# Layer 1's last sums on VectorE and GpSimd behind the last anchor tiles, their reads issued at once, and the anchors' rows read on ScalarE's queue

## The chip, the cores and the metric

The kernel runs on one core of a Trainium2 chip. The metric is the device time of one execution in microseconds (us). Before the change three executions took 1198.98, 1211.15 and 1212.76 us, with a median of 1211.15 us. A fourth execution, the profiled one, took 1202.78 us; its span from first to last instruction is 1200.6 us.

## What is computed

Two transformer layers run over x of shape (8, 256, 256), that is 2048 tokens of width 256. Each layer adds a cross-attention over 120 context rows and then a mixture of experts. Only the end of layer 1's mixture is touched by this change:

```python
# layer 1, per token of x (2048 tokens, 256 wide)
topidx = top 6 of 32 experts, tw = their normalised weights * 0.2
routed = sum over the 6 of tw * (silu(x @ w_gate[e]) * (x @ w_up[e])) @ w_down[e]
shared = silu(x @ shared_w_gate) * (x @ shared_w_up) @ shared_w_down
lg     = topidx[:, 0] // 2                        # one of 16 anchors
anchor = (silu(x @ anchor_w_gate[lg]) * (x @ anchor_w_up[lg])) @ anchor_w_down[lg]
out    = routed + shared + 0.1 * anchor
x      = x + out
```

So the last step adds to each token's row of x (which already holds the attention's and the shared expert's part) six rows of routed results and one row of the anchor's result.

## The kernel before

The program is written engine by engine, with every wait on a semaphore written out. Instructions of one engine run in the order of the code, and a wait holds up everything behind it on that engine. The tokens lie as 16 tiles of 128 (`NT = 16`) in the SBUF tile `X`, 256 numbers a token.

**Expert tiles.** Tokens of layer 1 are sorted by expert into tiles of 128 rows in DRAM (`buf1`). There are 160 such tiles (`NTL`): 128 routed ones and 32 of anchors. `tile_order` puts an anchor tile behind every fourth routed one from the 48th on and leaves 13 anchor tiles for the end. Index 146 is the last routed tile, `ROUTED` is 147, and indices 147 to 159 are anchors. For each tile i the loop does the following, each engine some tiles behind the one before:

- SyncE (SP) loads the tile's rows (`bx1_load`, `BX` or a piece of `R`), seven tiles ahead. The row's place comes from a table by a register load.
- TensorE (PE) transposes them (L304, L305). VectorE (DVE) copies the transpose to `XT` (L1410) and finds each row's destination `DI` and weight `WC` (`matches`, L1395 to L1403).
- PE multiplies by the gate and up weights (L656). ScalarE (ACT) applies silu (`SL`, L1134), DVE multiplies (`AC`, L1656), PE transposes (L665), ACT copies (`AT`, L1140), and PE multiplies by the down weights (L672).
- ACT scales the result by the weight (`yt_out`, L1087) into one of six buffers. GpSimd (POOL) scatters it by an indirect DMA (`put_back`, L884): rows of routed tiles go to `yb1` (six rows a token), those of anchor tiles to `yba` (one row a token).

**Last sums.** When all routed tiles are done (`all_back(E0 + ROUTED - 1)`), SP reads `yb1` back into SBUF with `yf_load(n)`, n from 0 to 7, each two token tiles (1.5 MB, 6 KB a row). The place `YF` is where the routed weights lay. From n = 4 on a read waits until DVE has done some of the sums. DVE runs `yf_add(n)` for one token tile in each step of the tile loop from i = 153 on, and the rest behind the loop: one addition of 768 numbers a partition, then three of 256. When all anchor results are in DRAM (`all_back(E0 + NTL - 1)`), SP reads them with four DMAs of 0.5 MB into `YA`. DVE adds them in four additions of 1024 numbers (L1666), and ACT writes each quarter of `X` out (L1145).

In the chip's trace the tiles `YF`, `YA`, `W1` and so on all bear the name `R`, since they are parts of one tensor. `yb1` is `yb` and `buf1` is `buf`.

Of the kernel before, what the change touches and what calls it, by code (L numbers as in the profile page):

```python
# [8 lines left out]
ALU = mybir.AluOpType  # L9
# [5 lines left out]
NT = 16  # L15
NB = 8
# [3 lines left out]
E0 = 64  # L20
# [9 lines left out]
EARLY = 3  # L30
NBX = 7
NYT = 6
BIG = 65536.0
SEG = 17
DUM = R1 * SEG
# [6 lines left out]
NTL = T1 + TA  # L42
# [45 lines left out]
ROUTED = ORDER.index(T1 - 1) + 1  # L88
# [15 lines left out]
class Chain:  # L104
# [14 lines left out]
    + [f"sc{i}" for i in range(6)] + ["z_b0", "z_y0", "z_dum"]  # L119
    + [f"ew{i}" for i in range(NEW // 2)] + [f"bx{i}" for i in range(NBX)] + [f"yt{i}" for i in range(NYT)]  # L120
    + [f"yl{i}" for i in range(3)] + [f"w1_{i}" for i in range(8)] + [f"wa_{i}" for i in range(4)]
    + ["pad_s", "pad_a", "pad_b"] + [f"yf{i}" for i in range(4)] + [f"ya{i}" for i in range(4)]

    + ["p_z", "p_va", "p_set", "p_y", "p_xc"]

    + ["s_kt", "s_tr", "s_q", "s_v", "s_s", "s_t", "s_o", "s_wo", "s_h2t", "s_rt", "s_ps"]
    + ["s_gu", "s_dn", "s_ta", "s_g", "s_t2", "s_y", "s_tot", "s_tab"]
# [3 lines left out]

    + ["dv", "d_ln", "d_h", "d_v", "d_cap", "d_mx", "d_pt", "d_cx", "d_x", "d_ln2", "d_hr", "d_lg", "d_sn", "d_sel", "d_ps"]
    + ["d_sum", "d_ri", "d_as", "d_add", "d_xt", "d_wc", "d_di", "d_ac", "d_kt", "d_bq", "d_xc", "d_tot", "d_pad", "d_cnt"]
    + ["d_tab", "d_te", "d_xf", "d_out"]
)


def build(nc, a, out):
# [10 lines left out]
    with ExitStack() as ctx:  # L149
# [11 lines left out]
        X = sb("X", [P, NT, D])  # L161
# [102 lines left out]
        YF = R[:, 0:NT * 1536].rearrange("p (s n) -> p s n", s=NT)  # L264
        YA = R[:, 24576:24576 + NT * D].rearrange("p (s n) -> p s n", s=NT)
# [7 lines left out]
        yv1p = yv1.rearrange("(n p) m -> p n m", p=P)  # L273
        yva = yba.rearrange("(n p) d -> p n d", p=P)
        buf1t = buf1.rearrange("(u p) r -> u p r", p=P)

        S = {name: ctx.enter_context(nc.semaphore(name)) for name in SIGNALS}
# [33 lines left out]
        def step(active):  # L311
            for g in list(active):
                if next(g, "end") == "end":
                    active.remove(g)
# [7 lines left out]
        def all_back(w, i):  # L322

            for k in range(i - NYT + 1, i + 1):
                s, n = result(k)
                w.wait_ge(f"yt{s}", 16 * n)
# [18 lines left out]
        def sweep(l, main, prepare, finish, first, behind, each=None):  # L345

            active = [first] if first is not None else []
            for u in range(-LEAD, NU + 2):
                if u % 4 == (-LEAD) % 4 and (u + LEAD) // 4 < NB:
                    active.append(prepare((u + LEAD) // 4))  # L350
                for slot in range(6):
                    main(u, slot)
                    if slot == 4 and u % 2 and 0 <= u - 2 < NU:
                        active.append(finish((u - 2) // 2, active))
                    step(active)
                    if u >= NU - 5 and slot % 2:
                        step(active)
                if each is not None and u > -LEAD + 1:
                    each()
            active.extend(behind)  # L360
            while active:
                step(active)

        block = ctx.enter_context(nc.Block())

# [311 lines left out]
        def _(e):  # L677
            w = Once(e, S)
# [127 lines left out]
            def yf_load(n):  # L806
                if n == 0:
                    w.wait_ge("s_y", E0 + ROUTED)
                    all_back(w, E0 + ROUTED - 1)
                e.dma_start(YF[:, 2 * n:2 * n + 2, :], yv1p[:, 2 * n:2 * n + 2, :]).then_inc(S[f"yf{n % 4}"], 16)  # L810

            for i in range(NBX):
                bx1_load(i)
            for i in range(NTL + 3):
                if i < 8:
                    pad(16 + 2 * i)
                if i + NBX < NTL:
                    bx1_load(i + NBX)
                if 10 <= i < 26:
                    pad(22 + i)  # L820
                n = i - ROUTED - 3
                if 0 <= n < NB:
                    if n >= 4:
                        w.wait_ge("d_xf", 2 * (n - 3))
                    yf_load(n)
            w.wait_ge("s_y", E0 + NTL)
            all_back(w, E0 + NTL - 1)
            for g in range(4):
                e.dma_start(YA[:, 4 * g:4 * g + 4, :], yva[:, 4 * g:4 * g + 4, :]).then_inc(S[f"ya{g}"], 16)


        @block.gpsimd
        def _(e):
            w = Once(e, S)
# [45 lines left out]
            def put_back(i, yb, bound):  # L880
                w.wait_ge("a_yt", i + 1)
                w.wait_ge("d_di", i + 1)
                j = i if i < E0 else i - E0
                e.indirect_dma_start(  # L884
                    out=yb[:, :], out_offset=bass.IndirectOffsetOnAxis(ap=DI[:, j:j + 1].bitcast(U32), axis=0),
                    in_=YTS[result(i)[0]], in_offset=None, bounds_check=bound, oob_is_err=False).then_inc(
                        S[f"yt{result(i)[0]}"], 16)
# [22 lines left out]
            for i in range(NTL):  # L910
                yb, bound = (yb1, 2048 * 6 - 1) if ORDER[i] < T1 else (yba, 2047)
                put_back(E0 + i, yb, bound)


        @block.scalar
        def _(e):
# [161 lines left out]
            def yt_out(i):  # L1078
                j = i if i < E0 else i - E0
                w.wait_ge("s_y", i + 1)  # L1080
                w.wait_ge("d_wc", i + 1)
                slot, n = result(i)
                if n > 1:
                    w.wait_ge(f"yt{slot}", 16 * (n - 1))
                if slot > 2:
                    w.wait_ge("s_dn", 4 * EARLY if i < E0 else 32)
                e.activation(YTS[slot], PS[:, 4 + j % 2, 0:256], ACT.Copy, scale=WC[:, j % 8:j % 8 + 1]).then_inc(  # L1087
                    S["a_yt"], 1)
# [35 lines left out]
            for i in range(NTL + 3):  # L1124
                if i in (0, 3):
                    w1_load(6 + i // 3)
                if i in (28, 32, 36, 40):
                    wa_load((i - 28) // 4)
                if 0 <= i - 1 < NTL:
                    j, wd = i - 1, width(i - 1)  # L1130
                    w.wait_ge("s_g", E0 + j + 1)
                    if j > 1:
                        w.wait_ge("d_ac", E0 + j - 1)
                    e.activation(SL[:, j % 2, 0:wd], PS[:, 2 + j % 2, 0:wd], ACT.Silu).then_inc(S["a_sl"], 1)  # L1134
                if 0 <= i - 2 < NTL:
                    j, wd = i - 2, width(i - 2)
                    w.wait_ge("s_t2", j + 1)
                    if j > 1:
                        w.wait_ge("s_y", E0 + j - 1)
                    e.copy(AT[0:wd, j % 2, :], PS[0:wd, 6 + j % 2, 0:P]).then_inc(S["a_at"], 1)  # L1140
                if 0 <= i - 3 < NTL:
                    yt_out(E0 + i - 3)
            for g in range(4):
                w.wait_ge("d_out", g + 1)
                e.dma_start(out_d[:, 4 * g:4 * g + 4, :], X[:, 4 * g:4 * g + 4, :]).then_inc(S["out"], 16)  # L1145
            w.wait_ge("out", 64)

# [2 lines left out]
        def _(e):  # L1150
# [479 lines left out]
            ready1 = set()  # L1630
            attention(1, route1, rows1, combine, [shared(1, 1, ready1, add1, range(4)), tables()], ready1, xc)

            def yf_add(n):
                yl = YF[:, n, :]
                w.wait_ge(f"yf{n // 2 % 4}", 16 * (n // 8 + 1))
                e.tensor_tensor(yl[:, 0:768], yl[:, 0:768], yl[:, 768:1536], ALU.add).then_inc(*dv.up())  # L1636
                t = dv.n
                w.wait_ge("dv", t)
                w.wait_ge("d_add", 32)
                e.tensor_tensor(X[:, n, :], X[:, n, :], yl[:, 512:768], ALU.add).then_inc(*dv.up())  # L1640
                e.tensor_tensor(yl[:, 0:256], yl[:, 0:256], yl[:, 256:512], ALU.add).then_inc(*dv.up())  # L1641
                w.wait_ge("dv", dv.n)
                e.tensor_tensor(X[:, n, :], X[:, n, :], yl[:, 0:256], ALU.add).then_inc(S["d_xf"], 1)

            w.wait_ge("d_tab", 1)
            for i in range(NTL + 3):
                if i < NTL:
                    xt_copy(E0 + i)
                    w.wait_ge(f"bx{(E0 + i) % NBX}", 16 * ((E0 + i) // NBX + 1))
                    matches(E0 + i, TE[:, ORDER[i]:ORDER[i] + 1])  # L1650
                if 0 <= i - 1 < NTL:
                    j, wd = i - 1, width(i - 1)
                    w.wait_ge("a_sl", E0 + j + 1)
                    if j > 1:
                        w.wait_ge("s_t2", j - 1)
                    e.tensor_tensor(AC[:, j % 2, 0:wd], SL[:, j % 2, 0:wd], PS[:, 2 + j % 2, wd:2 * wd], ALU.mult).then_inc(  # L1656
                        S["d_ac"], 1)
                if ROUTED + 6 <= i:
                    yf_add(i - ROUTED - 6)
            for n in range(NTL + 3 - ROUTED - 6, NT):  # L1660
                yf_add(n)
            for g in range(4):
                ns = slice(4 * g, 4 * g + 4)
                w.wait_ge(f"ya{g}", 16)
                w.wait_ge("d_xf", 4 * g + 4)
                e.tensor_tensor(X[:, ns, :], X[:, ns, :], YA[:, ns, :], ALU.add).then_inc(S["d_out"], 1)  # L1666

def by_partition(gate, up, down=None):

# [43 lines left out]
```

## Time and profile before

| | |
|---|---|
| three executions | 1198.98, 1211.15, 1212.76 us (median 1211.15) |
| profiled execution | 1202.78 us, span 1200.6 us |
| mean granted TensorE clock | 0.853 of full speed |
| busy in the span: PE, DVE, POOL, ACT | 81%, 55%, 44%, 41% |
| last slice of 30 us: DVE, DMA engines | 8 tenths, 7 tenths |

How to read the rows further down: times are microseconds from the span's start. A row of the timeline gives the start, the duration, the engine, the line of the code, the operation, and what is written `<-` what is read. In square brackets it gives how long the engine was idle before, and what ended that. A name like SPq or ACTq is the engine's queue issuing a DMA. PEclk is the TensorE clock granted, as a share of full speed.

### The profile page before, as it was taken

To read this page: it belongs to the slowest core of one execution; us is meant where nothing else is said; L and a number is where in the kernel's file an instruction comes from. 1 tells how busy PE (TensorE), PEld (TensorE's weight loads), DVE (VectorE), ACT (ScalarE), POOL (GpSimd) and SP (SyncE) were. 2 spreads that over 40 slices of the span, in tenths; PEclk is the share of its full clock that TensorE was granted. 3 is DMA by queue.
4 is the path that set the end of the run, shared out by engine and by line. 5 is a ranking of instruction groups with operands and counts; after the bars stand their busy time and mean duration, and the time that the engine had idled before them with its cause. 6 is when DMAs were issued, how large, how long until landed. Compare 5 with 4: busy or idle time off the path is not lost. (4 is left out here: it accounts for less than half of the span.)

```text
span 1200.6 us, 23250 instructions
## 1 busy us (share of the span) xinstructions
PE 977.6 (81%) x6378; PEld 710.8 (59%) x6378; DVE 657.3 (55%) x3257; ACT 493.3 (41%) x1608; POOL 531.6 (44%) x529
## 2 busy tenths in 40 slices
PE   6888888777897989788889887867578999998971
PEld 3566566545556878455666655643366777676740
DVE  3466556643323555447766666646345555555578
ACT  1476566533311433216644444322034545454430
POOL 1004455565501555499344334454044555555531
PEclk9588788866998999898987777667799999999965
DMA  9956531101506997465211111227476844444387
GB/s 309 351 198 208 192 109 52 33 18 30 207 19 209 363 362 227 184 222 199 107 63 63 55 59 68 73 77 301 165 256 204 244 150 137 144 145 129 90 335 267
DMA packets 115088, 198.82 MB, mean 166 GB/s; under 512 B 18712, under 2 KB 88685, under 8 KB 111890
## 3 DMA queue, kind: packets, MB, share of 16 engines
q1 hardware_dynamic: 61842, 112.33, 27.9%
q0 software_dynamic: 22272, 48.08, 10.9%
q10 hardware_dynamic: 30848, 36.92, 9.3%
q8 instruction: 55, 0.90, 0.3%
q14 instruction: 71, 0.58, 0.2%
HBM read 114.01 MB, written 98.98 MB: 177 GB/s over the span
## 5 line engine op out<-in xcount | busy, mean ns | idle before, releaser
L848 POOL DMA_INDIRECT buf<-R,RI x240 | 235.8, 982 | 353.2 <-ACT R L989 203.0
L656 PE MATMUL PS<-R,XT 128*128 x640 | 159.1, 373 | 12.6 <-DVE XT L1410 11.6
L884 POOL DMA_INDIRECT yb<-YT,DI x99 | 96.5, 975 | 155.3 <-DVE DI L1403 103.7
L1410 DVE COPY XT<-PS 128x256 f32<-128x256 f32 x224 | 94.8, 423 | 104.5 <-PE PS L305 90.0
L300 PE MATMUL PS<-R 128*128 128x256 f32 (+2 forms) x352 | 128.7, 508 | 23.9 <-DMA R<-in_ctxT 8.7
L884 POOL DMA_INDIRECT yb<-AS_,DI x93 | 90.6, 975 | 83.8 <-DVE DI L1403 41.0
L656 PEld LDWEIGHTS PS<-R,XT 128*128 128x128 f32 x640 | 108.0, 198 | 25.3 <-issue 17.8
L300 PEld LDWEIGHTS PS<-R 128*128 128x128 f32 (+1 forms) x352 | 76.6, 236 | 59.2 <-issue 35.7
L672 PE MATMUL PS<-R,AT 128*128 (+1 forms) x320 | 103.5, 407 | 0.0
L453 PE MATMUL PS<-C,R 128*120 128x128 f32 x512 | 92.7, 331 | 12.1 <-issue 10.3
L997 ACT COPY R<-PS 120x512 f32<-120x512 f32 x96 | 55.4, 582 | 107.5 <-remote 53.1
L989 ACT ACTIVATE R<-R,MX 128x120 f32<-128x120 f32 x256 | 80.0, 388 | 47.4 <-DVE MX L1239 33.4
L1134 ACT ACTIVATE SL<-PS 128x128 f32<-128x128 f32 (+1 forms) x160 | 42.6, 266 | 133.4 <-PE PS L656 110.8
L453 PEld LDWEIGHTS PS<-C,R 128*120 128x120 f32 x512 | 75.9, 171 | 29.8 <-issue 25.5
L437 PE MATMUL PS<-R 32*128 32x240 f32 x512 | 86.4, 451 | 6.1 <-issue 4.7
L989 ACT ACTIVATE R<-PS,MX 128x120 f32<-128x120 f32 x256 | 71.7, 368 | 16.0 <-DVE MX L1239 15.3
L300 PE MATMUL PS<-XT,R 128*128 128x128 f32 x512 | 70.8, 282 | 8.6 <-DVE XT L1410 8.6
L304 PE MATMUL PS<-C,R 128*128 128x128 f32 x160 | 50.8, 318 | 31.3 <-ACT R L966 18.8
L475 PE MATMUL PS<-R 120*32 120x128 f32 x1024 | 52.7, 337 | 24.8 <-ACT R L997 20.2
L300 PEld LDWEIGHTS PS<-XT,R 128*128 128x128 f32 x512 | 63.7, 195 | 12.8 <-DVE XT L1410 12.7
L1656 DVE TENSOR_TENSOR AC<-SL,PS 128x128 f32<-128x128 f32 (+1 forms) x160 | 43.5, 272 | 50.5 <-ACT SL L1134 35.1
L437 PEld LDWEIGHTS PS<-R 32*128 32x128 f32 x512 | 53.8, 220 | 26.5 <-issue 21.2
(203 smaller groups left out, 1931.4 us busy)
## 6 DMA issues: line engine op xcount, KB each, us to landing
R<-in_ew SPq DMA_DIRECT2D x64, 384.0 KB
BX<-buf SPq DMA_DIRECT2D x128, 140.0 KB
yb<-Z ACTq DMA_DIRECT2D x16, 1024.0 KB
R<-yb SPq DMA_DIRECT2D x16, 1024.0 KB, 4.8
R<-buf SPq DMA_DIRECT2D x96, 140.0 KB
R<-yb SPq DMA_DIRECT2D x8, 1536.0 KB, 10.3
R<-in_w SPq DMA_DIRECT2D x6, 1536.0 KB, 8.8
buf<-Z ACTq DMA_DIRECT2D x8, 1120.0 KB, 10.5
```

The lines of the kernel that those rows point to most:

```text
L300: m = e.matmul(out_, left, right, start=(i == 0), stop=(i == len(pairs) - 1))
L304: e.transpose(out_[:, 0:128], src[:, 0:128], ident)
L437: x = e.matmul(ps_scores(u, half)[:, 2 * c:2 * c + 2, :], QT[r, s, c, (n % 2) * P:(n % 2) * P + P], KALL[r, c, b, :, :], start=True, stop= ...
L453: x = e.transpose(PS[0:SK, 3 + half, i * P:i * P + P], SM[:, z, 4 * half + i, :], ident)
L475: x = e.matmul(PS[32 * q:32 * q + 32, 6, 256 * what + P * c:256 * what + P * c + P], left, PT[0:SK, 2 * (u % 2) + half, 2 * c + side, :], ...
L656: x = e.matmul(PS[:, 2 + j % 2, 0:2 * wd], XT[:, j % 3, k, :], src[:, bass.ds(regs[j], 1), k * 2 * wd:(k + 1) * 2 * wd].rearrange("p a n - ...
L672: e.matmul(PS[:, 4 + j % 2, 0:256], AT[0:wd, j % 2, :], src.rearrange("p a n -> p (a n)"), start=True, stop=True).then_inc(S["s_y"], 1)
L848: e.indirect_dma_start(out=(buf1 if l else buf0)[:, :], out_offset=bass.IndirectOffsetOnAxis(ap=RI[:, n % 6, k:k + 1].bitcast(U32), axis=0 ...
L884: e.indirect_dma_start(out=yb[:, :], out_offset=bass.IndirectOffsetOnAxis(ap=DI[:, j:j + 1].bitcast(U32), axis=0), in_=YTS[result(i)[0]], ...
L989: x = e.activation(SM[:, z, h, :], src[:, i, :], ACT.Exp, bias=MX[:, z, h:h + 1])
L997: e.copy(PT[0:SK, r, :, :], PS[0:SK, 3 + half, :].rearrange("p (h t) -> p h t", h=4)).then_inc(S["a_pt"], 1)
L1410: e.tensor_copy(XT[:, j % 3, :, :], two(PS[:, j % 2, 0:256])).then_inc(S["d_xt"], 1)
```

## The change

- DVE no longer sums during the tile loop. Behind the loop it handles 11 of the 16 token tiles with the new `last_sum`.
- POOL handles the other five (`BY_POOL`: 3, 6, 9, 12, 14) with the same function behind its last `put_back`.
- `last_sum` is the old four additions followed by the anchors' addition for that token tile alone (256 numbers instead of 1024 for four tiles). Before that last addition it waits for the anchors' read of its quarter.
- SP issues `yf_load(0)` as before, and `yf_load(1)` to `yf_load(7)` at once at i = 153, behind the last `bx1_load`. They no longer wait for sums; each has its own semaphore.
- The four reads of the anchors' rows move from SP's queue to ACT's, behind its last `yt_out`. The writes of the output wait for DVE's and POOL's counts.

```diff
+BY_POOL = (3, 6, 9, 12, 14)
...
+        def last_sum(e, w, own, name, n):
+            yl = YF[:, n, :]
+            w.wait_ge(f"yf{n // 2}", 16)
+            w.wait_ge("d_add", 32)
+            e.tensor_tensor(yl[:, 0:768], yl[:, 0:768], yl[:, 768:1536], ALU.add).then_inc(*own.up())
+            w.wait_ge(name, own.n)
+            e.tensor_tensor(X[:, n, :], X[:, n, :], yl[:, 512:768], ALU.add).then_inc(*own.up())
+            e.tensor_tensor(yl[:, 0:256], yl[:, 0:256], yl[:, 256:512], ALU.add).then_inc(*own.up())
+            w.wait_ge(name, own.n)
+            e.tensor_tensor(X[:, n, :], X[:, n, :], yl[:, 0:256], ALU.add).then_inc(*own.up())
+            w.wait_ge(f"ya{n // 4}", 16)
+            w.wait_ge(name, own.n)
+            return e.tensor_tensor(X[:, n, :], X[:, n, :], YA[:, n, :], ALU.add)
...
                 n = i - ROUTED - 3
-                if 0 <= n < NB:
-                    if n >= 4:
-                        w.wait_ge("d_xf", 2 * (n - 3))
-                    yf_load(n)
-            w.wait_ge("s_y", E0 + NTL)
-            all_back(w, E0 + NTL - 1)
-            for g in range(4):
-                e.dma_start(YA[:, 4 * g:4 * g + 4, :], yva[:, 4 * g:4 * g + 4, :]).then_inc(S[f"ya{g}"], 16)
+                if n == 0:
+                    yf_load(0)
+                if i == max(ROUTED + 3, NTL - NBX):
+                    for k in range(1, NB):
+                        yf_load(k)
...
                 put_back(E0 + i, yb, bound)
+            for n in BY_POOL:
+                last_sum(e, w, py, "p_y", n).then_inc(S["p_out"], 1)
...
+            all_back(w, E0 + NTL - 1)
             for g in range(4):
-                w.wait_ge("d_out", g + 1)
+                e.dma_start(YA[:, 4 * g:4 * g + 4, :], yva[:, 4 * g:4 * g + 4, :]).then_inc(S[f"ya{g}"], 16)
+            for g in range(4):
+                mine = sum(n < 4 * g + 4 for n in BY_POOL)
+                w.wait_ge("d_out", 4 * g + 4 - mine)
+                w.wait_ge("p_out", mine)
                 e.dma_start(out_d[:, 4 * g:4 * g + 4, :], X[:, 4 * g:4 * g + 4, :]).then_inc(S["out"], 16)
...
-                if ROUTED + 6 <= i:
-                    yf_add(i - ROUTED - 6)
-            for n in range(NTL + 3 - ROUTED - 6, NT):
-                yf_add(n)
-            for g in range(4):
-                ns = slice(4 * g, 4 * g + 4)
-                w.wait_ge(f"ya{g}", 16)
-                w.wait_ge("d_xf", 4 * g + 4)
-                e.tensor_tensor(X[:, ns, :], X[:, ns, :], YA[:, ns, :], ALU.add).then_inc(S["d_out"], 1)
+            for n in range(NT):
+                if n not in BY_POOL:
+                    last_sum(e, w, dv, "dv", n).then_inc(S["d_out"], 1)
```

**DVE, in the last anchor tiles.** Each step of the loop is the copy to `XT`, the three small instructions of `matches`, and the product `AC`. In the program before, from index 153 on, four sums stand behind the product (L1636 to L1643):

```order
L1656 TENSOR_TENSOR AC<-SL,PS 128x64
L1636 TENSOR_TENSOR R<-R 128x768
L1640 TENSOR_TENSOR X<-X,R 128x256
L1641 TENSOR_TENSOR R<-R 128x256
L1643 TENSOR_TENSOR X<-X,R 128x256
L1410 COPY XT<-PS 128x256
L1395 SCALAR_TENSOR_TENSOR JK,DF<-BX,TE 128x8
```

In the changed program the loop ends first. The sums follow the last two products, five to a token tile (L370 to L378; the last is the anchors' row):

```order
L1430 COPY XT<-PS 128x256
L1415 SCALAR_TENSOR_TENSOR JK,DF<-R,TE 128x8
L1420 SCALAR_TENSOR_TENSOR JK,WC<-R,TE 128x8
L1423 TENSOR_SCALAR DI<-DF 128x1
L1664 TENSOR_TENSOR AC<-SL,PS 128x64 x2
L370 TENSOR_TENSOR R<-R 128x768
L372 TENSOR_TENSOR X<-X,R 128x256
L373 TENSOR_TENSOR R<-R 128x256
L375 TENSOR_TENSOR X<-X,R 128x256
L378 TENSOR_TENSOR X<-X,R 128x256
```

So ten of the sixteen groups of sums moved out of the steps of the loop to behind it. Five of the sixteen are gone from DVE, as are its four large additions at the end.

**POOL, behind its last scatter of anchor rows.** Before, POOL ended with that scatter (`yba` is where the anchors' rows go). Now the following stands behind it, five times in all:

```order
L897 DMA yba<-YT,DI 2048x256 x3
L897 DMA yba<-AS_,DI 2048x256
L370 TENSOR_TENSOR R<-R 128x768
L372 TENSOR_TENSOR X<-X,R 128x256
L373 TENSOR_TENSOR R<-R 128x256
L375 TENSOR_TENSOR X<-X,R 128x256
L378 TENSOR_TENSOR X<-X,R 128x256
```

POOL thus runs its sums while DVE runs its own.

**SP's queue, at its end, in the changed program.** `R<-yb` is a read of the routed results (L826), `R<-buf` a load of a tile's rows (L819), and the rest is the register load of that tile's place:

```order
L826 DMA R<-yb 128x2x1536
L803 TENSOR_LOAD TU
L803 ISA x2
L819 ISA
L819 DMA R<-buf 128x280
L803 TENSOR_LOAD TU
L803 ISA x2
L819 ISA
L819 DMA R<-buf 128x280
L826 DMA R<-yb 128x2x1536 x7
```

The second read moved behind the last tile load. The reads of `yba`, which were the last on this queue, now stand on ACT's queue between its last `yt_out` and its writes of the output.

## Rows read from the trace of the kernel before

**Rows 1.** Timeline of DVE, end: where its sums begin and end
```profile
1152.22 0.96 DVE L1636 TENSOR_TENSOR R<-R 128x768 f32<-128x768 f32 x1 [3.55 <-DMA R<-yb]
...
1191.30 4.62 DVE L1666 TENSOR_TENSOR X<-X,R 128x1024 f32<-128x1024 f32 x4
```
**Rows 2.** Timeline of DVE: one token tile's four sums, and the next's first
```profile
1180.69 0.95 DVE L1636 TENSOR_TENSOR R<-R 128x768 f32<-128x768 f32 x1
1181.67 0.42 DVE L1640 TENSOR_TENSOR X<-X,R 128x256 f32<-128x256 f32 x1
1182.02 0.42 DVE L1641 TENSOR_TENSOR R<-R 128x256 f32<-128x256 f32 x1
1182.47 0.42 DVE L1643 TENSOR_TENSOR X<-X,R 128x256 f32<-128x256 f32 x1
1182.81 0.95 DVE L1636 TENSOR_TENSOR R<-R 128x768 f32<-128x768 f32 x1
```
**Rows 3.** Windows: us, busy PE, PEld, DVE, ACT, POOL, PEclk, DMA share, GB/s
```profile
1160.00:1162.00 2.00, 2.00 (x9) 1.26 (x7) 2.00 (x9) 0.47 (x1) 0.27 (x1) 0.50 1.04 427
...
1178.00:1180.00 2.00, 0.00 (x0) 0.00 (x0) 1.93 (x5) 0.00 (x0) 0.00 (x0) 0.50 0.98 400
1180.00:1182.00 2.00, 0.00 (x0) 0.00 (x0) 1.93 (x4) 0.00 (x0) 0.00 (x0) 0.50 0.11 37
```
**Rows 4.** Timeline of POOL's scatters: anchor tiles 147, 151 and the last, 159
```profile
1143.60 0.98 POOL L884 DMA_INDIRECT yba<-AS_,DI  x1 [0.30 <-issue]
1150.98 0.98 POOL L884 DMA_INDIRECT yba<-YT,DI  x1 [0.31 <-issue]
...
1176.40 0.98 POOL L884 DMA_INDIRECT yba<-AS_,DI  x1 [0.30 <-issue]
```
**Rows 5.** Timeline of SP's and ACT's queues: the reads and the writes at the end
```profile
1145.11 0.39 SPq L810 DMA_DIRECT2D R<-yb  x1
1148.92 25.80 SPq L810 DMA_DIRECT2D R<-yb  x6
1181.93 2.01 SPq L829 DMA_DIRECT2D R<-yba  x4
1192.55 3.78 ACTq L1145 DMA_DIRECT2D out<-X  x4
```
**Rows 6.** One line's issues: from issue to landing, for `yba` and for `out`
```profile
DMA to landing us min/median/max: 4.0/5.5/6.9
DMA to landing us min/median/max: 3.0/3.7/4.2
```
**Rows 7.** DMA queues, 872 to 874 us: packets, MB, share of 16 engines
```profile
q10 hardware_dynamic: 70, 0.70, 86.2%
q1 hardware_dynamic: 83, 0.09, 13.4%
```
**Rows 8.** DMA queues, 1164 to 1168 us
```profile
q1 hardware_dynamic: 278, 1.61, 98.1%
```
**Rows 9.** Timeline of POOL, layer 0's sums: a token tile beside DVE's, one without
```profile
507.19 3.25 POOL L901 TENSOR_TENSOR R<-R 128x512 f32<-128x512 f32 x2
...
516.70 2.35 POOL L898 TENSOR_TENSOR R<-R 128x1024 f32<-128x1024 f32 x1
519.13 2.08 POOL L901 TENSOR_TENSOR R<-R 128x512 f32<-128x512 f32 x2
521.29 0.73 POOL L904 TENSOR_TENSOR X<-X,R 128x256 f32<-128x256 f32 x1
```
**Rows 10.** Timeline of DVE, layer 0's sums: the first alone, the second beside POOL
```profile
503.29 1.15 DVE L1437 TENSOR_TENSOR R<-R 128x512 f32<-128x512 f32 x2
504.47 0.42 DVE L1440 TENSOR_TENSOR X<-X,R 128x256 f32<-128x256 f32 x1
...
508.22 2.50 DVE L1437 TENSOR_TENSOR R<-R 128x512 f32<-128x512 f32 x2
510.75 0.83 DVE L1440 TENSOR_TENSOR X<-X,R 128x256 f32<-128x256 f32 x1
```

More of the change, by code:

```diff
@@ L121 @@
     + [f"yl{i}" for i in range(3)] + [f"w1_{i}" for i in range(8)] + [f"wa_{i}" for i in range(4)]
-    + ["pad_s", "pad_a", "pad_b"] + [f"yf{i}" for i in range(4)] + [f"ya{i}" for i in range(4)]
-    + ["p_z", "p_va", "p_set", "p_y", "p_xc"]
+    + ["pad_s", "pad_a", "pad_b"] + [f"yf{i}" for i in range(8)] + [f"ya{i}" for i in range(4)]
+    + ["p_z", "p_va", "p_set", "p_y", "p_xc", "p_out"]
     + ["s_kt", "s_tr", "s_q", "s_v", "s_s", "s_t", "s_o", "s_wo", "s_h2t", "s_rt", "s_ps"]
@@ L133 @@
     + ["d_sum", "d_ri", "d_as", "d_add", "d_xt", "d_wc", "d_di", "d_ac", "d_kt", "d_bq", "d_xc", "d_tot", "d_pad", "d_cnt"]
-    + ["d_tab", "d_te", "d_xf", "d_out"]
+    + ["d_tab", "d_te", "d_out"]
 )
@@ L809, in yf_load @@
                     all_back(w, E0 + ROUTED - 1)
-                e.dma_start(YF[:, 2 * n:2 * n + 2, :], yv1p[:, 2 * n:2 * n + 2, :]).then_inc(S[f"yf{n % 4}"], 16)
+                e.dma_start(YF[:, 2 * n:2 * n + 2, :], yv1p[:, 2 * n:2 * n + 2, :]).then_inc(S[f"yf{n}"], 16)
             for i in range(NBX):
@@ L1631, in _ @@
             attention(1, route1, rows1, combine, [shared(1, 1, ready1, add1, range(4)), tables()], ready1, xc)
[L1633 to L1643, printed above, removed]
             w.wait_ge("d_tab", 1)
```

## Prediction, made before the changed kernel ran

> **What bounds the kernel now.** The change touches only what happens after about 1145 us of a span of 1200.6 us, so I read the end of the timeline of DVE first. DVE waits 3.55 us for the first read of routed results, starts its sums at 1152.22 and is busy without a gap until its four large additions end at 1195.92 (1191.30 + 4.62) [rows 1]. Then the last write of the output lands, 4.7 us later. One token tile's four sums take 2.12 us, from 1180.69 to 1182.81 [rows 2]. The work in those 43.7 us is 16 x 2.12 = 33.9 us of sums, 4.6 us of large additions, and about 5 us of the last anchor tiles' own instructions, which stand between the first ten groups of sums. So DVE sets the end now.
>
> Next I read the windows. The DMA engines are full (0.98 to 1.04) and move 400 to 427 GB/s until 1180, then drop to 0.11 [rows 3]. The routed reads are 8 x 1.5 MB = 12.6 MB; at 410 GB/s they take 31 us from their first issue at 1145.11 [rows 5]. DVE's sums therefore run just inside a second bound, the DMA engines, and the reads cannot be over before about 1180 however early they are issued. The anchors' reads start at 1181.93, behind the last scatter, which POOL issued at 1176.40 [rows 4, 5].
>
> **What the change does, step by step.** The sum is made on the profiled execution.
>
> *Reads issued at once.* DMA engines are already full from 1148 to 1180. Reads 4 to 7 waited for sums, but read 7 still ended with the engines full. I count 0 us. All sixteen windows of 2 us from 1148 to 1180 stand at 0.96 or more (two of them are in [rows 3]), so there is no gap that an earlier issue could close. Nor does read 1, now behind the last tile load, cost anything: read 0 alone keeps the engines busy for 3.8 us.
>
> *Anchor tiles without sums.* DVE no longer holds them up. POOL's scatters of anchor tiles 147 to 151, before any sum, came every (1150.98 - 1143.60) / 4 = 1.85 us [rows 4]. Eight more put the last scatter at 1150.98 + 8 x 1.85 = 1165.8, issued in full by 1166.8, against 1177.4 before. Bounds: 1.28 us a tile (0.98 of one scatter and the 0.30 before it) gives 1162.2; the pace before with sums, (1176.40 - 1150.98) / 8 = 3.2 us, gives no gain.
>
> *The anchors' reads.* Before, they were issued 4.55 us after POOL had issued the last scatter (1177.38 to 1181.93), with the DMA engines still full for most of it. The same gap now gives 1171.3. In idle DMA engines the first quarter landed in 4.0 us [rows 6]: 1175.3. But now the engines are not idle: the routed reads hold them until 1180. How two queues share is to be seen at 872 to 874 us, where ACT's queue (q10) reads weights and SP's (q1) reads tile rows: 70 packets of 10 KB against 83 of 1.1 KB, and 0.70 against 0.09 MB [rows 7]. They share by packets, about one for one, so small packets get few bytes. A quarter of the anchors' rows is 512 packets of 1 KB. The routed reads' packets are of 6 KB and pass at 278 in 4 us, 14.4 ns each [rows 8]. So 512 x 14.4 ns = 7.4 us of waiting, 1.3 us for its own 0.5 MB, and some 2.5 us of the 4.0 that is no transfer make 11.2 us: 1182.5. The routed reads themselves end at about 1181.4 with this mixed in, and then nothing is in the way. I take **1182** for the first quarter, with 1175.3 and 1184 as bounds. The other three quarters follow within 5 us, ahead of need.
>
> *What waits for it.* `last_sum(0)` on DVE needs that quarter for its fifth addition, and everything else on DVE stands behind it. DVE is done with the anchor tiles near 1162, does four sums until 1164, and then waits about 18 us. Before, it was busy all this time. POOL likewise does four sums for token tile 3 and waits. This is where the gain of the earlier start goes: what was hidden under the reads now stands behind them.
>
> *The sums behind the wait.* On DVE alone a token tile costs 2.12 us, plus a fifth addition at 0.34 and the 0.10 for a wait on the one before (1182.47 against 1182.02 + 0.35) [rows 2]: 2.56 us. On POOL alone it is 1.84 for 768 numbers (between 2.35 for 1024 and 1.35 for 512), four times 0.73, and gaps of 0.08: 5.2 us [rows 9].
>
> *Both at once.* The trace has one token tile where both add SBUF tiles, near 507 to 511 us. DVE's three additions of 512, 256 and 256 numbers took 1.60 us alone (503.29 to 504.89) and 3.36 us beside POOL (508.22 to 511.58). POOL's two took 3.25 us in place of 2.08 [rows 9, 10]. So each slows the other: an addition waits until the other engine's is over. By numbers added, 1792 in a token tile against 1024 in that piece, DVE's token tile beside POOL is 3.36 x 1.75 = 5.9 us; I take 6.0. Bounds: 2.56 if they don't hinder each other, and 7.4 with nothing overlapped (0.95 + 4 x 0.42 on DVE, 1.84 + 4 x 0.73 on POOL) [rows 2, 9].
>
> The Trainium skill (SBUF — State Buffer, section "Who interferes with whom") states that a VectorE instruction with two SBUF inputs and a GpSimd instruction that reads SBUF exclude each other, the later one blocking fully. By that rule alone a pair would be the 7.4 us, and the total 5.6 us more than mine; the trace agrees that they block, but its 3.36 us shows that the fixed parts overlap.
>
> POOL has four token tiles left behind the wait. During these DVE also does four: 4 x 6.0 = 24.0 us. Six more on DVE alone are 6 x 2.56 = 15.4. The two fifth additions ahead are 0.8. Sum 40.2 us, so the last addition ends at 1182 + 40.2 = 1222.2. One output write of 0.5 MB then needs 0.2 to issue and 3.7 to land [rows 6] (before, it was 4.7 with the others queued ahead): **1226.1, which is 25.5 us over 1200.6**.
>
> The profiled execution would thus go from 1202.8 to 1228.3. The three others were 1199.0 to 1212.8; the mean of all four is 1206.5, which gives 1232, and the median 1211.15 gives 1236.7. I take 1231.
>
> **The rivals.**
>
> 1. *No hindrance between DVE and POOL*, since the one piece of evidence is short. Then DVE needs 0.4 + 10 x 2.56 = 26.0 behind the wait: 1182 + 26.0 + 3.9 = 1211.9, which is 11.3 us over, some 1214 for this execution. This is the one that ends as not slower, within 2%. It decides from a pair cost under about 5.6 us (25.5 less 4 x 0.4 is 24). Against it speak both engines' doubled times at the same moment.
> 2. *The anchors' reads get their share early* (1175.3 and not 1182): 6.7 us less, so 18.8 us over, some 1222. For it: the shares of rows 7 are for other transfers. Against: the packet counts are plain.
> 3. *Full exclusion*, 7.4 us a pair: 31 us over, some 1234.
> 4. *TensorE's clock falls to 1.2 GHz in the anchor tiles as it did before* (0.50 [rows 3], after PE had waited for DVE). At some 2.9 us a tile the last scatter is 1174.5, the reads are issued near 1180, and the quarter lands at 1184: 2 us more than forecast, as the wait is for the routed reads either way.
> 5. *Faster than before.* With both rival 1 and the quarter landed by 1170.7 the end is 1200.6 (1170.7 + 29.9). DVE's work does fall, from 38.5 us to 11 x 2.56 = 28.2. But it cannot begin in earnest at 1152 as now.
>
> **How the numbers follow.** Two per cent, about what a measurement of this kernel can tell from no change, is 24 us. The forecast, with rival 4 inside it, 0.66; rival 1, 0.13; rival 2, 0.12; rival 3, 0.06; rival 5, 0.03. The forecast's own range is 25.5 +/- 4, so it is over 24 in somewhat more than half of the cases: 0.38 slower, 0.28 within 2%. Rival 3 is slower; rivals 1 and 2 are within 2%. Together: slower 0.44, same 0.53, faster 0.03. The range runs from rival 1 on the profiled execution (1202.8 + 11.3, less 2 for its base) to the forecast with 4 more on the slowest of the four (1212.8 + 29): 1212 to 1241.
>
> **What would show it.** In the changed profile: the last scatter of anchor rows near 1166; DVE idle between some 1164 and 1182, ended by the anchors' read; the routed reads over near 1181; four of DVE's token tiles at about 6 us and the rest at 2.56; POOL's at 6 and not 5.2; the last addition near 1222. The forecast is wrong if the anchors' first quarter lands before 1178, or if DVE's additions keep to 0.42 us while POOL adds.

## The result, and the profile after

The changed kernel took 1237.79 us (median of four executions, 1231.91 to 1257.84) against 1210.59 us before. The ratio is 1.0228, with a 95% interval of 1.014 to 1.0317: slower, by 27.2 us. Whether it is slower by more than 2%, the interval leaves open. The ratio leaves out one execution of the changed kernel, 1257.84 us, as too far above its fastest, and the profiles of e7 and e10 further down were taken of such slow executions. The forecast was 1231 us with a range of 1212 to 1241.

The profiled execution has a span of 1237.1 us. To compare it with the 1200.6 us of before, both are cut where SP issues the first routed read. The code ahead of that point is the same in both. I call what follows it **the tail**.

| | first routed read | span | tail |
|---|---|---|---|
| before | 1145.11 | 1200.6 | 55.5 |
| after | 1154.74 | 1237.1 | 82.4 |

The tail grew by 26.9 us, about as much as the medians differ (27.2). The 9.6 us ahead of it are within what this part varies by: kernels with the code of before up to this point reached it at 1127.22, 1153.37 and 1155.31 us (e11, e8, e7 below), with tails of 55.0, 55.5 and 55.7.

Timeline of SP's and ACT's queues and of POOL's last scatter, changed kernel (start, duration, engine, line, operation, what ended the idle time before):

```profile
1154.74 0.39 SPq L826 DMA_DIRECT2D R<-yb  x1
1159.38 9.75 SPq L826 DMA_DIRECT2D R<-yb  x7
...
1180.09 0.98 POOL L897 DMA_INDIRECT yba<-AS_,DI  x1 [0.30 <-issue]
...
1186.07 3.60 ACTq L1160 DMA_DIRECT2D R<-yba  x4
1205.76 28.40 ACTq L1165 DMA_DIRECT2D out<-X  x4
```

The last scatter is issued by 1181.07, 26.3 us after the first routed read (before: 32.3, [rows 4, 5]). The anchors' reads follow 5.0 us later.

Timeline of DVE, changed kernel, from its last product of the tile loop on: the first token tile, one beside POOL, one alone, and the end:

```profile
1174.96 0.22 DVE L1664 TENSOR_TENSOR AC<-SL,PS 128x64 f32<-128x64 f32 x1 [2.29 <-ACT SL L1149]
1175.10 0.95 DVE L370 TENSOR_TENSOR R<-R 128x768 f32<-128x768 f32 x1
...
1176.88 0.43 DVE L375 TENSOR_TENSOR X<-X,R 128x256 f32<-128x256 f32 x1
1193.45 0.43 DVE L378 TENSOR_TENSOR X<-X,R 128x256 f32<-128x256 f32 x1 [16.15 <-DMA R<-yba]
1193.80 1.48 DVE L370 TENSOR_TENSOR R<-R 128x768 f32<-128x768 f32 x1
1195.31 1.91 DVE L372 TENSOR_TENSOR X<-X,R 128x256 f32<-128x256 f32 x1
1197.14 0.94 DVE L373 TENSOR_TENSOR R<-R 128x256 f32<-128x256 f32 x1
1198.11 0.83 DVE L375 TENSOR_TENSOR X<-X,R 128x256 f32<-128x256 f32 x1
1198.97 0.83 DVE L378 TENSOR_TENSOR X<-X,R 128x256 f32<-128x256 f32 x1
1199.72 1.48 DVE L370 TENSOR_TENSOR R<-R 128x768 f32<-128x768 f32 x1
...
1220.61 0.95 DVE L370 TENSOR_TENSOR R<-R 128x768 f32<-128x768 f32 x1
1221.59 0.42 DVE L372 TENSOR_TENSOR X<-X,R 128x256 f32<-128x256 f32 x1
...
1233.32 0.42 DVE L378 TENSOR_TENSOR X<-X,R 128x256 f32<-128x256 f32 x1
```

Timeline of POOL over the same time:

```profile
1193.50 0.96 POOL L378 TENSOR_TENSOR X<-X,R 128x256 f32<-128x256 f32 x1 [8.31 <-DMA R<-yba]
1194.42 2.51 POOL L370 TENSOR_TENSOR R<-R 128x768 f32<-128x768 f32 x1
1197.01 0.78 POOL L372 TENSOR_TENSOR X<-X,R 128x256 f32<-128x256 f32 x1
...
1200.35 2.51 POOL L370 TENSOR_TENSOR R<-R 128x768 f32<-128x768 f32 x1
```

Two losses are to be seen. DVE waits 16.15 us for the anchors' read, in which before it was summing without a gap [rows 1]. Then a token tile beside POOL takes 5.92 us (1193.80 to 1199.72), while one alone takes 2.6 us. POOL's token tile takes 5.93 (1194.42 to 1200.35) in place of the 5.2 estimated alone. The additions interlock: DVE's L372 from 1195.31 to 1197.22 spans the rest of POOL's addition of 768, which ends at 1196.93.

Windows of the changed kernel (us, busy PE, PEld, DVE, ACT, POOL, then PEclk, DMA share, GB/s):

```profile
1158.00:1160.00 2.00, 1.53 (x9) 0.76 (x8) 0.00 (x0) 0.44 (x1) 1.42 (x2) 1.00 1.00 342
1162.00:1164.00 2.00, 2.00 (x10) 1.26 (x10) 1.40 (x14) 0.89 (x4) 1.22 (x2) 0.68 1.05 429
1188.00:1190.00 2.00, 0.00 (x0) 0.00 (x0) 0.00 (x0) 0.00 (x0) 0.00 (x0) 0.50 0.98 398
1190.00:1192.00 2.00, 0.00 (x0) 0.00 (x0) 0.00 (x0) 0.00 (x0) 0.00 (x0) 0.50 1.08 358
1196.00:1198.00 2.00, 0.00 (x0) 0.00 (x0) 2.00 (x2) 0.00 (x0) 1.92 (x3) 0.50 0.09 31
```

The DMA engines are full until 1196 and then nearly idle, while DVE still adds for 38 us and POOL for 22. Before, adding and reading ran side by side [rows 3]. TensorE's clock fell to half here too, near 1163, after PE had been idle for part of 1158 to 1162.

### The profile page after: what moved, and what is told of

It reads as the page before. It is cut to its first block and busy times, and to the rows that moved or that the text cites. A ratio compares the mean times of both kernels' runs of the same rounds, so it can differ in the third digit from the quotient of the medians.

```text
span 1237.1 us, 23271 instructions
## 1 busy us (share of the span) xinstructions
PE 980.5 (79%) x6378; PEld 712.5 (58%) x6378; DVE 665.1 (54%) x3244; ACT 493.2 (40%) x1608; POOL 557.6 (45%) x554
## 5 line engine op out<-in xcount | busy, mean ns | idle before, releaser
L672 PEld LDWEIGHTS PS<-R,XT 128*128 128x128 f32 x640 | 108.2, 198 | 20.2 <-issue 13.1
L1012 ACT COPY R<-PS 120x512 f32<-120x512 f32 x96 | 55.5, 583 | 103.6 <-PE PS L469 56.2
L305 PE MATMUL PS<-C,R 128*128 128x128 f32 x160 | 51.0, 319 | 37.1 <-ACT R L981 18.9
L1004 ACT ACTIVATE R<-PS,MX 128x120 f32<-128x120 f32 x256 | 71.6, 369 | 21.3 <-DVE MX L1259 20.8
L453 PEld LDWEIGHTS PS<-R 32*128 32x128 f32 x512 | 53.0, 222 | 19.9 <-issue 15.3
## 6 DMA issues: line engine op xcount, KB each, us to landing
R<-yb SPq DMA_DIRECT2D x8, 1536.0 KB, 21.7
```

The lines of the kernel that those rows point to most:

```text
L305: e.transpose(out_[:, 0:128], src[:, 0:128], ident)
L453: x = e.matmul(ps_scores(u, half)[:, 2 * c:2 * c + 2, :], QT[r, s, c, (n % 2) * P:(n % 2) * P + P], KALL[r, c, b, :, :], start=True, stop= ...
L672: x = e.matmul(PS[:, 2 + j % 2, 0:2 * wd], XT[:, j % 3, k, :], src[:, bass.ds(regs[j], 1), k * 2 * wd:(k + 1) * 2 * wd].rearrange("p a n - ...
L1004: x = e.activation(SM[:, z, h, :], src[:, i, :], ACT.Exp, bias=MX[:, z, h:h + 1])
L1012: e.copy(PT[0:SK, r, :, :], PS[0:SK, 3 + half, :].rearrange("p (h t) -> p h t", h=4)).then_inc(S["a_pt"], 1)
```

## Experiments

All kernels but three are the kernel before or after with one edit: e10 has two edits, e9 and e12 are a version of their own, and e11 is the kernel before. e2, e3 and e6 leave out part of the computation. Times within one execution are compared by the tail. "Quarter" is the moment at which DVE's first anchors' addition starts, counted from the first routed read. Spans of different rows are not to be compared, as the kernel before had medians of 1189.5 us beside e1 to e4, 1210.3 beside e5 to e8, 1207.6 beside e9 and e10, and 1179.8 (one execution) beside e11 and e12. Each ratio is to the kernel before in the same group.

| run | span | tail | quarter | ratio to before (95%) |
|---|---|---|---|---|
| after | 1237.1 | 82.4 | 38.7 | 1.0228 (1.014 to 1.0317) |
| e1 no POOL | 1220.3 | 81.2 | 38.5 | 1.0196 (1.0112 to 1.028) |
| e2 POOL's share left out | 1192.8 | 68.6 | 38.7 | 1.009 (1.0049 to 1.013) |
| e3 POOL only writes | 1194.1 | 67.0 | 37.1 | one execution |
| e4 anchors last | 1205.9 | 75.7 | | 1.0102 (0.999 to 1.0214) |
| e5 reads on SP | 1235.0 | 81.8 | 38.1 | one execution |
| e6 half the routed reads | 1212.8 | 70.9 | 27.2 | one execution |
| e7 before, at once | 1211.0 | 55.7 | | 0.9992 (0.9938 to 1.0046) |
| e8 before, reads on ACT | 1208.9 | 55.5 | | 0.998 (0.9904 to 1.0057) |
| e9 pairs | 1211.0 | 50.3 | | 1.0012 (0.9977 to 1.0047) |
| e10 no POOL, anchors last | 1220.8 | 59.0 | | 1.0042 (1.0005 to 1.0079) |
| e11 before again | 1182.2 | 55.0 | | one execution |
| e12 pairs again | 1184.1 | 50.7 | | one execution |

### e1: GpSimd's share back on VectorE

```diff
-BY_POOL = (3, 6, 9, 12, 14)
+BY_POOL = ()
```

> The changed kernel with GpSimd's share put back on VectorE: all 16 token tiles are summed by VectorE behind the last anchor tile. Theory (VectorE and GpSimd exclude each other while both add, so that GpSimd's share saves nothing): behind the wait for the anchors' read come 0.4 + 15 x 2.61 = 39.6 us, against 40.3 us in the changed kernel (1193.45 to 1233.74). The end stays where it is within 2 us, at 1.02 of the kernel before. Rival (GpSimd's share is a help, only too small a one): five token tiles more on VectorE cost 5 x 2.6 = 13 us, 1.033 of before.

Timeline of DVE in this run, the end of its wait:

```profile
1177.59 0.42 DVE L378 TENSOR_TENSOR X<-X,R 128x256 f32<-128x256 f32 x1 [19.37 <-DMA R<-yba]
```

Behind the wait DVE needs 39.3 us (1177.59 to 1216.93) with all 16 token tiles, against 40.3 with eleven of them in the changed kernel. The tail is 81.2 against 82.4. GpSimd's five token tiles thus save nothing; the rival's 13 us are not there. The ratio, 1.0196, is the 1.02 of the theory.

### e2: GpSimd's share left out

```diff
-            for n in BY_POOL:
-                last_sum(e, w, py, "p_y", n).then_inc(S["p_out"], 1)
...
-                w.wait_ge("p_out", mine)
```

> The changed kernel without GpSimd's five token tiles: they are summed by nobody, VectorE still does its eleven. This leaves out part of the computation. Theory (each of VectorE's four token tiles beside GpSimd takes 5.92 us where it takes 2.61 alone): 4 x 3.3 + 0.4 = 13.7 us less than the changed kernel, so about 1.011 of before, and all VectorE additions of 256 numbers at 0.42 us. Rival (the additions are slow at that time for another reason, such as the DMA engines writing to SBUF): no change, 1.02.

Timeline of DVE in this run, the token tile behind the wait:

```profile
1162.93 0.42 DVE L378 TENSOR_TENSOR X<-X,R 128x256 f32<-128x256 f32 x1 [20.87 <-DMA R<-yba]
1163.28 0.95 DVE L370 TENSOR_TENSOR R<-R 128x768 f32<-128x768 f32 x1
1164.27 0.42 DVE L372 TENSOR_TENSOR X<-X,R 128x256 f32<-128x256 f32 x1
1164.61 0.42 DVE L373 TENSOR_TENSOR R<-R 128x256 f32<-128x256 f32 x1
1165.06 0.42 DVE L375 TENSOR_TENSOR X<-X,R 128x256 f32<-128x256 f32 x1
```

The same additions take 0.95 and 0.42 us, and the tail is 13.8 us shorter than after's (13.7 expected). So the slow additions are POOL's doing. This run shows the hindrance most directly, since the quarter came at 38.7 in both.

### e3: GpSimd writes and does not read

```diff
             for n in BY_POOL:
-                last_sum(e, w, py, "p_y", n).then_inc(S["p_out"], 1)
+                yl = YF[:, n, :]
+                w.wait_ge(f"yf{n // 2}", 16)
+                for wd in (768, 256, 256, 256):
+                    e.memset(yl[:, 0:wd], 0.0).then_inc(*py.up())
+                    w.wait_ge("p_y", py.n)
+                w.wait_ge(f"ya{n // 4}", 16)
+                e.memset(yl[:, 0:256], 0.0).then_inc(S["p_out"], 1)
```

> The changed kernel with GpSimd's additions replaced by memsets of the same widths, which read nothing. This leaves out part of the computation. If the engines exclude each other only over reads of SBUF, VectorE's token tiles beside it take 2.6 us and the time from the first routed read's issue to the end falls by about 13.7 us, from 82.4 to 69 us. If any GpSimd work on SBUF holds VectorE up, its additions are still longer than 0.42 us while GpSimd writes.

Timelines of this run: POOL's memsets after the wait, and DVE's additions beside them:

```profile
1164.55 1.84 POOL L930 MEMSET R<- 128x768 f32 x4
...
1164.55 0.95 DVE L370 TENSOR_TENSOR R<-R 128x768 f32<-128x768 f32 x1
1165.54 0.42 DVE L372 TENSOR_TENSOR X<-X,R 128x256 f32<-128x256 f32 x1
```

DVE's additions keep their 0.95 and 0.42 us while POOL writes SBUF. The tail is 67.0 us, 1.6 shorter than e2's, and the quarter came 1.6 us earlier. So GpSimd's writes to SBUF are not what holds VectorE's two-input additions up. That its reads are is what is left, by exclusion: a memset differs from an addition in its arithmetic too, and no run has GpSimd read without writing. The Trainium skill (SBUF — State Buffer, section "Who interferes with whom") puts it on the reads: a VectorE instruction with two SBUF inputs contends with a GpSimd instruction that reads SBUF, not with one that only writes it. This run agrees as to the writes, 0.42 us beside the memsets against 0.83 to 1.91 beside additions.

### e4 and e10: the anchors' additions last, with and without GpSimd

```diff
-                    last_sum(e, w, dv, "dv", n).then_inc(S["d_out"], 1)
+                    four_sums(e, w, dv, "dv", n)
+            for n in range(NT):
+                if n not in BY_POOL:
+                    anchor_sum(e, w, dv, "dv", n).then_inc(S["d_out"], 1)
```

`four_sums` and `anchor_sum` are the two parts of `last_sum`; POOL's loop is split in the same way. e10 has `BY_POOL = ()` as well.

> The changed kernel with the anchors' additions behind all other sums on both engines: first four sums for each token tile, then the anchors' rows. Theory (the sums stand behind the wait for the anchors' read only because of their order): VectorE starts at about 20 us after the first routed read's issue and does not stop. 2.8 token tiles alone, five beside GpSimd at some 5.1 us, 3.2 alone at 2.12 and eleven last additions make about 42 us, and the end is some 66 us after that issue instead of 82.4: 16 us less, 1.01 of before. Rival (the routed reads are what is waited for): the end moves by less than 6 us.

> The changed kernel with the anchors' additions last and all 16 token tiles on VectorE. Theory (GpSimd's additions cost VectorE more than they save): from its first sum VectorE needs 16 x 2.12 + 16 x 0.35 = 39.5 us, against 46 us in the version with GpSimd's share and the anchors last, so about 6 us less, with a tail of 63 to 69 us depending on when the tiles end. Rival (GpSimd helps once nothing waits): 5 token tiles more at 2.47 us are 12 us more than the 46.

DVE does not wait for the anchors' read in either. From its first sum to its last addition e4 takes 45.0 us (1155.54 to 1200.50) and e10 takes 39.6 (1177.13 to 1216.74, 39.5 expected). So even where nothing waits for that read, five token tiles on POOL cost 5.4 us rather than save any.

The tails missed what was expected: 75.7 us where I had 66, and 59.0 where I had 63 to 69. Most of it is when the sums begin. I had about 20 us after the first routed read; e4's started at 25.3 and e10's at 15.3. The rest of e4's miss is 3 us more of sums (45.0 for 42) and an output of 5.4 us. The anchor tiles ran at half clock in e4 (0.50 from 1132 on, two microseconds after that read) and at full clock in e10. Rows of e10's windows, from the end of its tile loop and behind it:

```profile
1168.00:1170.00 2.00, 1.40 (x7) 0.84 (x8) 0.78 (x6) 0.00 (x0) 1.15 (x2) 1.00 1.08 399
1170.00:1172.00 2.00, 1.26 (x7) 0.62 (x6) 1.04 (x8) 1.10 (x6) 0.00 (x0) 1.00 1.01 412
...
1174.00:1176.00 2.00, 2.00 (x12) 1.27 (x12) 0.92 (x7) 0.39 (x3) 1.23 (x2) 1.00 1.00 418
1180.00:1182.00 2.00, 0.00 (x0) 0.00 (x0) 1.93 (x5) 0.00 (x0) 1.39 (x3) 0.50 1.02 418
```

PE was idle for as much of 1168 to 1172 here as of 1158 to 1162 in the changed kernel's profile, and yet the clock stayed at 1.00 here and fell there. Why it falls in one execution and not in another is open.

So part of e4's distance to e10 (16.7 us) goes with the clock (10.0, the later start) and part is POOL's (5.4). Against e1, the order alone brought e10 22.2 us. Of these, 19.4 are the wait in e1's row, which e10 does not have, and 1.6 are e10's earlier start.

### e5 and e6: what the anchors' read waits for

e5 moves the four reads back to SP, behind the routed reads:

```diff
                     for k in range(1, NB):
                         yf_load(k)
+            w.wait_ge("s_y", E0 + NTL)
+            all_back(w, E0 + NTL - 1)
+            for g in range(4):
+                e.dma_start(YA[:, 4 * g:4 * g + 4, :], yva[:, 4 * g:4 * g + 4, :]).then_inc(S[f"ya{g}"], 16)
```

e6 issues only four of the eight routed reads, and what waited for a later one waits for the fourth:

```diff
-            w.wait_ge(f"yf{n // 2}", 16)
+            w.wait_ge(f"yf{min(n // 2, NB // 2 - 1)}", 16)
...
-                    for k in range(1, NB):
+                    for k in range(1, NB // 2):
                         yf_load(k)
```

> The changed kernel with the anchors' reads on SyncE's queue, behind the eight routed reads, as before the change. Theory (on ScalarE's queue they share packet by packet with the routed reads and gain no time, since the first quarter lands only when the routed reads are over): the first quarter lands at the same 38 to 39 us after the first routed read's issue, and the tail from that issue to the end stays at 82 us within 2. Rival (the move to ScalarE's queue is itself what delays the anchors' rows): the quarter lands at least 4 us earlier, at 34 us or less, and the tail shortens by as much.

> The changed kernel with only the first four of eight routed reads; the sums of the other token tiles use what lies in SBUF. This leaves out part of the computation. Theory (the anchors' first quarter waits for the routed reads to pass): the routed reads end about 15 us earlier, the scatter and the quarter land in idle DMA engines, the quarter at the last scatter's end plus 2 and 4 us, which is 25 to 32 us after the first routed read's issue instead of 38.5, and the tail is 7 to 13 us shorter than 82.4. Rival (the anchors' read is late because of the tiles and the scatter alone): 38 us again.

On SP's queue the quarter came at 38.1 us and the tail was 81.8: the queue makes no difference. With half the routed reads the quarter came at 27.2 us. Timelines of e6, ACT's queue and DVE:

```profile
1165.18 2.06 ACTq L1160 DMA_DIRECT2D R<-yba  x4
...
1169.10 0.43 DVE L378 TENSOR_TENSOR X<-X,R 128x256 f32<-128x256 f32 x1 [8.58 <-DMA R<-yba]
```

There the reads were issued 1.2 us after the last scatter (1163.96 to 1165.18) instead of 5.0, and DVE's wait ended 3.9 us after that, in place of 7.4. The other 4.2 us of the 11.5 are a last scatter issued by 22.1 us and not 26.3. Alone these would not have brought the quarter forward: in e2 the last scatter was issued earlier still (by 20.8 us), and with all eight routed reads the quarter came at 38.7. The tail fell by 11.5 us to 70.9, just as much as the quarter came earlier. So it is the routed reads in the DMA engines that the quarter waits for.

e1, e2 and e3 test this too. Their tiles ended at different times, so ACT issued the anchors' reads 27.7, 25.8 and 24.0 us after the first routed read (31.3 in after). The quarter came at 38.5, 38.7 and 37.1 all the same, so reads issued up to 7.3 us earlier gained 1.6 at most. DMA queues in e2, from 1152 to 1156, from 1156 to 1160, and in the two microseconds behind that, with both queues reading (packets, MB, share of 16 engines):

```profile
q1 hardware_dynamic: 253, 1.47, 90.4%
q10 hardware_dynamic: 149, 0.15, 11.0%
...
q1 hardware_dynamic: 237, 1.41, 86.9%
q10 hardware_dynamic: 233, 0.24, 17.2%
...
q10 hardware_dynamic: 499, 0.50, 74.4%
q1 hardware_dynamic: 51, 0.22, 27.8%
```

From 1156 to 1160, 237 packets of 6 KB stand against 233 of 1 KB: one for one, as in [rows 7], and so a seventh of the bytes. When the routed reads run out, the anchors' rows pass at once.

### e7 and e8: the two DMA edits alone, on the kernel before

```diff
-                if 0 <= n < NB:
-                    if n >= 4:
-                        w.wait_ge("d_xf", 2 * (n - 3))
-                    yf_load(n)
+                if n == 0:
+                    yf_load(0)
+                if i == max(ROUTED + 3, NTL - NBX):
+                    for k in range(1, NB):
+                        yf_load(k)
```

That is e7, with a semaphore for each read. e8 moves the four anchors' reads of the kernel before to ACT's queue, in front of its output writes.

> The kernel before with its routed reads issued at once and nothing else changed. Theory (the DMA engines were full anyway): same as before within 0.5%, the tail from the first routed read's issue to the end 55.5 us within 1.5. Rival (reads in one go crowd out the tiles' loads and scatters): the tail is 3 us or more longer, with the last scatter later than 31 us after that issue.

> The kernel before with the anchors' reads on ScalarE's queue and nothing else changed. Theory: VectorE's sums end the kernel and the anchors' rows come ahead of need on either queue, so same as before within 0.5% and a tail of 55.5 us within 1.5. Rival (ScalarE's queue delays them): VectorE waits for the anchors' rows behind its sums and the tail grows by 2 us or more.

Tails of 55.7 and 55.5 us, ratios of 0.9992 and 0.998 with intervals that hold 1: neither edit costs or brings anything that these runs can tell where VectorE's sums stay in the tile loop. The last scatter of e7 was issued by 32.5 us, as before (32.3), so the rival's mark of 31 us says nothing.

### e9, e11 and e12: two token tiles in one addition

This version was meant to beat both. It is e7 and e8 together, and each addition handles a whole routed read:

```diff
-                yl = YF[:, n, :]
-                w.wait_ge(f"yf{n // 2}", 16)
-                e.tensor_tensor(yl[:, 0:768], yl[:, 0:768], yl[:, 768:1536], ALU.add).then_inc(*dv.up())
+                yl, x = YF[:, 2 * k:2 * k + 2, :], X[:, 2 * k:2 * k + 2, :]
+                w.wait_ge(f"yf{k}", 16)
+                e.tensor_tensor(yl[:, :, 0:768], yl[:, :, 0:768], yl[:, :, 768:1536], ALU.add).then_inc(*dv.up())
...
-                if ROUTED + 6 <= i:
-                    yf_add(i - ROUTED - 6)
+                if i in (157, 159, 161):
+                    yf_add((157, 159, 161).index(i))
```

> A version built on the kernel before, with everything on VectorE: each addition handles the two token tiles of one routed read (1536 and 512 numbers a partition instead of 768 and 256), three of the eight pairs in the tile loop (from index 157 on, when the first read has landed), five behind it, the reads at once and the anchors' reads on ScalarE's queue. By 1.04 ns a number and 0.08 an instruction a pair takes 3.7 us instead of 4.24, which is 4.3 us less work, and VectorE does not hold the loop up at index 153. The tail from the first routed read's issue to the end is about 52 us instead of 55.5, 0.997 of before. If the routed reads bound it, it is 49 us at best. Rival (VectorE's work is not what sets the end): 55.5 us as before.

> The kernel before once more, for a second look at its two parts: the time until SyncE issues the first routed read, and the tail from there to the end. The tail is expected at 55.5 us within 1; what differs between executions by 10 us and more should lie ahead of that read (1145 us in the first look).

> The version with two token tiles per addition once more. If its gain in the tail is real, the tail is again 50 to 51 us, against 55.5 of the kernel before run beside it. If the one profile was a chance, the tail is within 1 us of 55.5. Should the part ahead of the first routed read be 4 us or more longer than in the kernel before beside it, something in that part gives the gain back.

Timeline of DVE in e9, one pair and the start of the next:

```profile
1179.32 1.75 DVE L1636 TENSOR_TENSOR R<-R 128x1536 f32<-128x1536 f32 x1
1181.11 0.69 DVE L1639 TENSOR_TENSOR X<-X,R 128x512 f32<-128x512 f32 x1
1181.72 0.68 DVE L1640 TENSOR_TENSOR R<-R 128x512 f32<-128x512 f32 x1
1182.44 0.69 DVE L1642 TENSOR_TENSOR X<-X,R 128x512 f32<-128x512 f32 x1
1183.05 1.75 DVE L1636 TENSOR_TENSOR R<-R 128x1536 f32<-128x1536 f32 x1
```

A pair takes 3.73 us as worked out (3.7), and the tail is 50.3 us (some 52 expected), and 50.7 in the second profile, against 55.5 and 55.0: 4.3 to 5.2 us shorter, both times. Yet the whole kernel is no faster: the ratio is 1.0012 (0.9977 to 1.0047). In the second profile the first routed read came at 1133.43 us, and at 1127.22 in the kernel before beside it, which is 6.2 us later in code that is the same. The interval allows a gain of 0.23% at most, 2.8 us, less than the 4.3 to 5.2 of the tails. If the other executions have tails like the profiled ones, chance alone therefore explains this badly, and something ahead of the tail gives the gain back. What that is stays open. None of these versions is shown to beat the kernel before.

## Why the prediction was right

The time, 1237.8, lies 6.8 us above the forecast and inside the range. Slower by more than 2% had 0.44 and within 2% had 0.53. The measured 2.28% is on the first side, which had the smaller chance of the two, and its interval reaches down to 1.4%. The change itself was forecast at 25.5 us and measured at 27.2 by the medians. The other 5.1 of the 6.8 us are the base, which the forecast took at 1205.5 and which came out at 1210.59. The upper end of the range is by its own sum 1241.8 and not 1241. By its own steps, with times counted from the first routed read (1145.11 in the forecast):

- **Reads issued at once cost nothing.** Right: e7, within 0.5%.
- **Anchor tiles without sums.** The forecast had 1.85 us a tile and the last scatter issued at 21.7 us. It was 26.3. The pace was 2.83 us in the last tiles (POOL's scatters from 1166.30 to 1174.80 are three such steps), at a granted clock of 0.50 (1.2 GHz). This was rival 4, named with its 2.9 us a tile. Before, the pace was 2.94 us (POOL's scatters from 1158.80 to 1173.49 are five such steps) with VectorE busy without a gap. Taking the sums away uncovered a second limit just behind it. It depends on the execution: with the clock at 1.00 through all anchor tiles, e2, e3, e5 and e6 had the last scatter issued by 20.8, 19.2, 22.1 and 22.1 us, around the forecast's 21.7, and e4, at 0.50 from the start, by 31.8. Of the 4.6 us only about two reached the quarter, as the rival said they would.
- **The quarter at 36.9 us.** It was 38.7. The mechanism held in all its parts: e5, e6 and e2's packets. The wait behind the last scatter was 5.0 us, not 4.55. This term was 1.8 us too small. From issue to landing the sum had 11.2 us; in e2 and e3, where the routed reads ran on beside it, it was 13.0 and 13.1.
- **VectorE waits about 18 us.** 16.15, because it came to the wait later.
- **A pair at 6.0 us.** 5.92, four times in a row. This was the term with the widest bounds (2.56 to 7.4) and the thinnest evidence, three additions of VectorE's and two of GpSimd's in layer 0. On such evidence a miss of only 0.08 us is in part luck. Rival 1 (no hindrance) and rival 3 (nothing overlapped) both fall with it. By the exclusive lock of the Trainium skill (SBUF — State Buffer, section "Who interferes with whom") alone it would have been 7.4. The trace agrees that the two engines hold each other up, but its 5.92 us show that some part of each instruction overlaps with the other's.
- **Alone 2.56 us.** 2.58 to 2.65 (1220.61 to 1223.26 is the longest). Six of them took 16.2 us with the first addition still held up by POOL (1217.50 to 1233.74), where the sum had 15.4.
- **Behind the wait 40.2 us.** 40.3 (1193.45 to 1233.74). So close a match is partly errors that cancel: the last six were 0.8 us longer, the four beside POOL 0.3 shorter, and the fifth addition ahead of them took 0.35 where the sum had 0.8 for two. The output took 3.4 us and not 3.9.
- **25.5 us in all.** 26.9 in the tail.

Rival 2, an early share for the anchors' reads, is refuted by the quarter's 38.7 us. Rival 5 needed it by 25.6, which not even e6 reached (27.2).

Of the 26.9 us, GpSimd's share accounts for about one, since e1 without it has nearly the same tail (81.2). The loss is that VectorE's sums moved from beside the reads to behind them, and that the help meant to make up for it takes from VectorE as much as it gives. With the anchors' additions last and all sums on VectorE (e10), 3.5 us of it is left in the profiled execution, whose anchor tiles ran at full clock, and 0.42% (some 5 us) over nine executions.

## What to carry to other kernels

Work that fills a wait for a transfer should not be placed behind something that waits for the end of that transfer: here one late operand at the fifth of five additions held up all additions of every later token tile, for 16 to 21 us. Before giving VectorE's two-input additions to GpSimd, look for a place in the trace where both add SBUF tiles, and take the pair's cost from there; here 11 + 5 token tiles took as long as 16 + 0. A small read on one engine's queue, started while a large one is queued on another's, got one packet for each of the large read's and so few of the bytes; it landed at 37.1 to 38.7 us, against 38.1 behind the large read on the same queue (e5).

## What I had not expected of the hardware

- The part of the kernel ahead of the first routed read, the same code in all versions, took from 1124.20 us (e2) to 1161.83 us (e10) in single profiles. A difference of 1% between single executions of this kernel says nothing; the tail, cut at an event, repeated within 0.5 us in the two kernels that were profiled twice (55.5, 55.0; 50.3, 50.7).
- With the DMA engines full, ACT saw the last scatter as landed, and issued the anchors' reads, 5.0 us after the scatter; with them nearly idle it took 1.2 us (e6).
- GpSimd's memsets of 768 and three times 256 numbers took 1.84 us together (e3), and its addition of 768 numbers with nothing of VectorE's beside it 1.82 us.
